# Reciprocals of the softmax sums as scaled fp16 pairs, one context piece loaded to another place, and a new order of work

## The reference

```
x = x + tanh(g_xattn) * ( softmax(mask(q kT * 64^-0.5)) v @ W_o + b_o )
      q = layernorm(x) @ W_q ; k = ctx @ W_k ; v = ctx @ W_v ; 8 heads of 64
x = x + tanh(g_ffn) * ( bitlinear(gelu(bitlinear(layernorm(x), w1, b1)), w2, b2) )
bitlinear(x, w, b): rmsnorm(x) rounded to 8 bits by its row's maximum,
                    w rounded to -1, 0, 1 by mean(|w|), product scaled back, + b
```

## Time and profile before

| | |
|---|---|
| time, median of 3 runs | 1135.02 us (1132.27 to 1136.66) |
| the profiled execution | 1132.84 us, span 1131.0 us |
| PE busy | 1033.3 us (91% of the span) |
| DVE busy | 909.8 us (80%) |
| POOL busy | 862.6 us (76%) |
| ACT busy | 794.7 us (70%) |
| DMA queue of the kernel | 74.6% of 16 engines |

### The profile page before, as it was taken

The page is one execution under the profiler, slowest core; times in us unless marked ns, Lnnn a source line. Parts: engine busy times, 40 slices in busy tenths (PEclk is TensorE's granted clock), DMA queues, the critical chain, the costliest instruction groups (busy, mean ns, idle before and its releaser), DMA issues.

```text
span 1131.0 us, 23832 instructions
## 1 busy us (share of the span) xinstructions
PE 1033.3 (91%) x8372; PEld 610.6 (54%) x8372; DVE 909.8 (80%) x1768; ACT 794.7 (70%) x1389; POOL 862.6 (76%) x767
## 2 busy tenths in 40 slices
...
GB/s 258 256 188 157 198 108 176 136 166 143 152 161 126 194 130 129 148 154 181 119 179 132 154 149 138 173 120 182 128 157 133 154 185 106 138 132 131 141 61 65
DMA packets 480005, 170.77 MB, mean 151 GB/s; under 512 B 458256, under 2 KB 460048, under 8 KB 479504
## 3 DMA queue, kind: packets, MB, share of 16 engines
q1 hardware_dynamic: 479888, 169.25, 74.6%
...
...
## 4 chain that ended last, share of the span: by engine, by line
PE 55%; POOL 16%; DVE 10%; issue 8%; DMA 6%; ACT 4%; SPq 1%; DVEq 0%; ACTq 0%; POOLq 0%
PE ps_g L544 29%; POOL p L984 8%; PE ps_g L641 7%; PE ps_g L597 6%; PE ps_s L574 6%; PE ps_g L633 5%; DMA hqt<-hq 4%; POOL p L979 2%; PE ps_g L585 2%; DVE prob L701 2%; DVE hq L835 1%; DVE xa L744 1%; ACT prob L881 1%; DMA xt<-xh 1%; POOL h_sb L1047 1%
## 5 line engine op out<-in xcount | busy, mean ns | idle before, releaser
L984 POOL TENSOR_TENSOR p<-prob,p 112x750 f16<-112x750 f32 x256 | 416.4, 1638 | 9.0 <-ACT p L888 4.9
L701 DVE CUSTOM_DVE_ANT_0 prob<-ps_s,mbias 112x750 f32<-112x750 f32 x256 | 235.6, 930 | 55.8 <-PE ps_s L574 52.9
L881 ACT ACTIVATE prob<-prob,rmin 112x750 f32<-112x750 f32 x256 | 233.6, 913 | 26.1 <-DVE rmin L701 25.8
L544 PE MATMUL ps_g<-ctx,wk 128*128 128x375 f16 x1152 | 203.2, 327 | 19.8 <-POOL ctx L995 18.1
L544 PE MATMUL ps_g<-wv,ctx 128*128 128x512 f16 (+1 forms) x864 | 204.0, 382 | 9.2 <-POOL ctx L995 6.2
L574 PE MATMUL ps_s<-k_sb,q_sb 64*112 64x375 f16 x1536 | 150.2, 328 | 17.0 <-DVE rmin L701 16.7
L544 PEld LDWEIGHTS ps_g<-ctx,wk 128*128 128x128 f16 x1152 | 108.3, 98 | 105.3 <-issue 35.5
L544 PEld LDWEIGHTS ps_g<-wv,ctx 128*128 128x128 f16 (+1 forms) x864 | 88.5, 104 | 96.5 <-issue 9.3
L888 ACT ACTIVATE p<-prob 112x750 f16<-112x750 f32 x160 | 129.5, 819 | 5.5 <-DMA pt<-p 4.6
L574 PEld LDWEIGHTS ps_s<-k_sb,q_sb 64*112 64x112 f16 x1536 | 90.5, 127 | 74.6 <-issue 41.9
L979 POOL CAST p<-prob 112x750 f16<-112x750 f32 x96 | 104.2, 1086 | 28.1 <-ACT prob L881 27.9
...
## 6 DMA issues: line engine op xcount, KB each, us to landing
...
pt<-p SPq DMA_TRANSPOSE x256, 3.9
...
```

The costliest lines, as they stand in the source:

```text
L544: mm = nc.tensor.matmul(out, lhs, rhs, start=(m == 0), stop=(m == len(steps) - 1))
L701: nc.vector.tensor_tensor_reduce(prob[:, (b * NU + n) % PROBS, :].rearrange("p (c k) -> p c k", c=2), ps_s[0:HT, n % 2, :, 0:CH], mbias[:, ...
L881: nc.scalar.activation(prob[:, (b * NU + n) % PROBS, :], prob[:, (b * NU + n) % PROBS, :], ACT.Exp, bias=rmin[:, n:n + 1], scale=-1.0, acc ...
L984: nc.gpsimd.tensor_tensor(p16[:, u % HILO, 1, 0:J], prob[:, (b * NU + n) % PROBS, :], p16[:, u % HILO, 0, 0:J], ALU.subtract).then_inc(s[" ...
```

## The change

Four things change.

1. `R:n` is now four per batch instead of eight. Each takes four reciprocals and then writes them, times 1024, as an fp16 high half and an fp16 low half (`rr16`). That is three dependent DVE instructions instead of one, each waiting for the one before it by a semaphore.
2. `PV:n` spreads the two halves instead of the one fp32 number: eight fp16 products that add up in pairs, instead of four fp32 products. The identity is fp16 and holds 1/1024.
3. The third context piece of batch 0 goes into a free part of `pt`, with a semaphore of its own, and no longer waits for POOL.
4. All tables of the order are new.

```
-                    nc.vector.reciprocal(rrec[:, 2 * n:2 * n + 2], rsum[:, 2 * n:2 * n + 2])\
-                        .then_inc(s["recips"], 1)
+                    of = slice(4 * n, 4 * n + 4)
+                    need(dve, "expd", b, 4 * n + 3)
+                    need(dve, "weighted", b - 1, n)
+                    nc.vector.reciprocal(rrec[:, of], rsum[:, of]).then_inc(s["recips_f"], 1)
+                    need(dve, "recips_f", b, n)
+                    nc.vector.tensor_scalar(rr16[:, 0, of], rrec[:, of], RS, None, ALU.mult).then_inc(s["recips_hi"], 1)
+                    need(dve, "recips_hi", b, n)
+                    nc.vector.scalar_tensor_tensor(out=rr16[:, 1, of], in0=rrec[:, of], scalar=RS, in1=rr16[:, 0, of],
+                                                   op0=ALU.mult, op1=ALU.subtract).then_inc(s["recips"], 1)
...
                     for m in range(2 * n, 2 * n + 2):
                         at = 256 + half_of(b, m) * HT
-                        for e in range(2):
-                            nc.tensor.matmul(g[e * DH:(e + 1) * DH, at:at + HT],
-                                             rrec[:, 2 * m + e:2 * m + e + 1].to_broadcast([HT, DH]),
-                                             ident[0:HT, 0:HT], start=True, stop=True)
+                        for a in range(2):
+                            for e in range(2):
+                                nc.tensor.matmul(g[e * DH:(e + 1) * DH, at:at + HT],
+                                                 rr16[:, a, 2 * m + e:2 * m + e + 1].to_broadcast([HT, DH]),
+                                                 ident[0:HT, 0:HT], start=(a == 0), stop=(a == 1))
...
+        def ctx_place(c):
+            return pt_words[:, 3 * WCH:3 * WCH + J] if c == KC - 1 else ctx_f[:, c % 2, :]
...
-                    need(sp, "ctx_lo", 0, c - 2)
-                    sp.dma_start(ctx_f[:, c % 2, :], ctx_d[b, :, n, :]).then_inc(d_ctx[c % 2], 16)
+                    if c >= KC:
+                        need(sp, "ctx_lo", 0, c - 2 if c > KC + 1 else 1)
+                    sp.dma_start(ctx_place(c), ctx_d[b, :, n, :]).then_inc(d_ctx[2 if c == KC - 1 else c % 2], 16)
...
 START = listed("""
-    MB:0:0 PW:0:0 CX:0:0 LC:0:0 CX:1:0 PD:0:0 N1:0:0 XN:0:0 XH:0:0 LC:1:0 LM:0:0 LX:0:0 XH:1:0 PD:1:0 CX:2:0 PW:1:0
+    CX:0:0 N1:0:0 LX:0:0 XN:0:0 LC:0:0 CX:1:0 PW:0:0 XH:0:0 XH:1:0 CX:2:0 PW:1:0 K:0:0 N1:0:1 KL:0:0 KL:1:0 XN:0:1
```

More of the change, by code:

```diff
@@ L46 @@
 VS = 8.0
+RS = 1024.0
 QSCALE = -(DH ** -0.5) / WS
@@ L137 @@
[L137 to L151, removed]
@@ new lines @@
+    Q:1:0 KL:3:0 PD:2:0 XH:1:1 WB:0:0 LX:0:1 M:1:0 WA:1:0 WA:2:0 K:4:0 XT:0:0 KL:4:0 S:0:0 XT:1:0 V:0:0 LM:0:0
+    WB:1:0 WA:3:0 M:2:0 E:0:0 L:0:0 WL:0:0 WA:4:0 WL:2:0 WB:2:0 WL:1:0 VL:0:0 E:1:0 VL:1:0 K:5:0 WL:3:0 M:3:0
+    WL:4:0 WL:5:0 WA:5:0 S:1:0 KL:5:0 WL:6:0 L:1:0 KL:6:0 LX:0:2 V:1:0 WL:7:0 WB:3:0 E:2:0 WA:6:0 K:6:0 WA:7:0
+    V:2:0 WM:0:0 PD:3:0 LC:0:1 VL:2:0 E:3:0 WL:8:0 H:0:0 PW:3:0 H:1:0 K:7:0 V:3:0 WQ:0:0 KL:7:0 WR:0:0 LC:1:1
+    BD:0:0 WB:4:0 WR:1:0 V:4:0 WR:2:0 WL:9:0 WR:3:0 WQ:1:0 V:5:0 WR:4:0 WQ:2:0 CX:0:1 CX:1:1 E:4:0 WB:5:0 WQ:3:0
@@ new lines @@
+    M:4:0 Q:2:0 WL:12:0 S:2:0 WL:15:0 WA:8:0 VL:3:0 N1:0:2 H:2:0 WB:6:0 WA:9:0 WL:10:0 M:5:0 WL:13:0 WG:0:0 E:5:0
+    WR:5:0 LC:2:1 WL:11:0 Q:3:0 L:2:0 WA:10:0 S:3:0 WQ:4:0 WB:7:0 S:4:0 WQ:5:0 H:3:0 QL:2:0 CX:2:1 WR:6:0 WA:11:0
+    M:6:0 WR:7:0 WA:12:0 WA:13:0 L:3:0 M:7:0 WL:14:0 WQ:6:0 V:0:1 T:0:0 VL:4:0 VL:5:0 L:4:0 H:4:0 XN:0:2 K:0:1
+    K:1:1 T:1:0 XT:0:1 QL:3:0 H:5:0 WA:14:0 VL:0:1 M:8:0 M:9:0 S:5:0 R:0:0 KL:0:1 WM:1:0 KL:1:1 QL:0:1 WA:15:0
+    M:10:0 R:1:0 T:2:0 WQ:7:0 XT:1:1 M:11:0 VL:1:1 E:6:0 WQ:8:0 E:7:0 QL:1:1 T:3:0 VL:2:1 M:12:0 H:6:0 T:4:0 WR:8:0
@@ new lines @@
+    L:5:0 LM:0:1 M:13:0 Q:0:1 LC:0:2 T:5:0 WB:8:0 H:7:0 Q:1:1 E:8:0 T:6:0 WB:9:0 L:6:0 T:7:0 R:2:0 H:8:0 WB:10:0
+    E:9:0 WB:11:0 PA:0:0 V:1:1 T:8:0 WQ:9:0 V:2:1 H:9:0 T:9:0 PV:0:0 L:7:0 L:8:0 L:9:0 WB:12:0 WQ:10:0 KL:2:1 S:6:0
+    E:10:0 WR:9:0 H:10:0 T:10:0 WR:10:0 E:11:0 E:12:0 M:14:0 K:2:1 K:3:1 T:11:0 WQ:11:0 L:10:0 WB:13:0 M:15:0
+    WR:11:0 S:7:0 H:11:0 K:4:1 L:11:0 KL:3:1 WQ:12:0 M:0:1 KL:4:1 PA:1:0 E:13:0 WR:12:0 H:12:0 MB:0:1 PV:1:0 L:12:0
+    E:14:0 QL:2:1 PL:0:0 WQ:13:0 M:1:1 T:12:0 BD:1:0 R:3:0 H:13:0 E:15:0 L:13:0 WB:14:0 Q:2:1 T:13:0 WB:15:0
@@ L156 @@
+    WR:13:0 S:0:1 E:0:1 KL:5:1 H:14:0 PL:1:0 K:5:1 H:15:0 WQ:14:0 WR:14:0 L:14:0 H:0:1 M:2:1 VL:3:1 V:3:1 KL:6:1
+    E:1:1 PA:2:0 L:15:0 K:6:1 M:3:1 V:4:1 VL:4:1 E:2:1 L:0:1 L:1:1 LR:1:0 S:1:1 M:4:1 PV:2:0 M:5:1 KL:7:1 H:1:1
+    XH:0:2 PA:3:0 K:7:1 T:14:0 XH:1:2 CX:0:2 V:5:1 T:15:0 T:0:1 WQ:15:0 LM:0:2 PL:2:0 E:3:1 WR:15:0 LC:1:2 H:2:1
+    XB:1:0 S:2:1 VL:5:1
 """, 0)
@@ new lines @@
+    PL:0:-1 H:9:-1 L:7:-1 E:10:-1 M:10:-1 T:6:-1 T:7:-1 F1:2:-2 GE:0:-2 F1:3:-2 GS:0:-2 R:1:-1 LR:0:-1 T:8:-1
+    L3:1:-2 L:8:-1 M:11:-1 H:10:-1 XQ:1:-2 T:9:-1 T:10:-1 S:6:-1 L4:1:-2 E:11:-1 PV:1:-1 H:11:-1 L:9:-1 T:11:-1
+    L:10:-1 S:7:-1 HT:0:-2 GM:0:-2 G2:0:-2 M:12:-1 GI:0:-2 M:13:-1 PA:1:-1 L:11:-1 L:12:-1 G3:0:-2 M:14:-1 R:2:-1
+    E:12:-1 H:12:-1 M:15:-1 F1:4:-2 F1:5:-2 R:3:-1 E:13:-1 H:13:-1 E:14:-1 F1:6:-2 F1:7:-2 T:12:-1 T:13:-1 T:14:-1
+    L:13:-1 PA:2:-1 PL:1:-1 L:14:-1 H:14:-1 T:15:-1 E:15:-1 LR:1:-1 PV:2:-1 F2:0:-2 H:15:-1 L:15:-1 GE:1:-2 PL:2:-1
@@ L173 @@
+    GM:1:-2 HT:1:-2 XB:0:-1 G2:1:-2 GI:1:-2 GS:1:-2 PV:3:-1 PL:3:-1 XQ:0:-1 PA:3:-1 GE:0:-1 G3:1:-2 O:0:-1 XB:1:-1
+    L2:0:-1 L3:0:-1 O:1:-1 L4:0:-1 XQ:1:-1 L2:1:-1 GS:0:-1 L3:1:-1 L4:1:-1 GE:1:-1 F2:1:-2 F1:0:-1 F1:1:-1 F1:2:-1
+    HT:0:-1 F1:3:-1 F1:4:-1 F1:5:-1 F1:6:-1 F1:7:-1 GM:0:-1 G2:0:-1 HT:1:-1 GI:0:-1 GM:1:-1 G2:1:-1 G3:0:-1 G3:1:-1
+    F2:0:-1 GI:1:-1 GS:1:-1 F2:1:-1
 """, NB)
```

47 lines of the change are left out of this document (16 added, 31 removed), and 57 rows, old and new, of tables (SLOTS, STAGE_OF_ITEM).

## The result

The changed kernel takes 1151.2 us (median of 4 runs, 1149.4 to 1157.3) against 1135.8 us before: a ratio of 1.015, 95% interval 1.011 to 1.020. It is slower by some 15 us, where 8 us less was forecast. The profiled execution of the changed kernel is the 1157.3 us one (span 1155.5), so it shows a few us more than the median does.

What follows compares the result with a forecast made beforehand. TensorE was taken to set the pace of the two-tile batches. Terms of -8.5, +4.5, -2 and -2 summed to -8.0 us, from 1132.8 to 1124.8 for the profiled execution, median 1127 us, range 1116 to 1142.

Steps and rivals of the forecast that it cites:

- the order in the middle: New item order in the middle batches: costed at nothing, as TensorE's items keep nearly the same neighbours.
- What bounds the kernel: Eleven two-tile batches between 1 and 14: TensorE sets the pace, busy 65.56 of a 65.65 us period.
- Term 1: TensorE's products spreading the reciprocals: fp16 takes 0.27 us a unit instead of 0.43, 8.5 us less (0 to 13).
- third of the rivals: Spread products on TensorE: an fp16 pair still takes 0.10 us, so no gain there; 1135.5 us, chance 0.10.
- Term 2: VectorE's new fp16-half operations, stretched beside GpSimd: 0.4 us a two-tile batch, 4.5 us more in all (0 to 19).
- VectorE becomes the bound: Two-tile batches: reciprocal items stretched by 1.6 us make VectorE set a 67.2 us period; 1146.5 us, chance 0.18.
- Term 3: Start: third context piece issued earlier, first product near 14.5 us, 3.5 sooner; 2 us less (0 to 4).
- Term 4: Last batch: `M:14` straight after `G3`, hidden rows' transpose sooner; 2 us less (4 less to 1 more).

Runs made afterwards that it cites:

- experiment 2: The changed kernel with fp32 reciprocals and spread products; new orders, four-column items and context place stay: 1110.9 us (0.978).
- experiment 4: The changed kernel without VectorE's computation of the low halves, which are set to zero once; TensorE's products stay: 1104.5 us (0.972).
- experiment 8: The changed kernel with one fp16 reciprocal straight from VectorE and one product in place of a pair, no low half: 1099.1 us (0.967).
- experiment 1: The changed kernel with only VectorE's item `R:3` moved behind `PA:2` in the last row of the order table: 1121.6 us (0.987).
- experiment 9: The changed kernel with the low half's operation replaced by a same-size reciprocal that nobody reads, low halves zero: 1105.6 us (0.974).
- experiment 5: The kernel before with only the first batch's third context piece loaded to its own place at once: 1135.05 us (0.999).

## Why the prediction was wrong, point by point

From the runs, before to changed: 2 us less by merging the items, 22 less by the new orders (with the context place), 40 more by the pairs. My sum had 0 for the order in the middle, -4 for start and tail, and -4 for the pairs (-8.5 and +4.5). So two terms were far off, in opposite directions, and the 15 us in the result are what is left of them.

**What bounds the kernel.** That TensorE sets the pace was right. The step from there was not: "its 0.1 us of idle in a two-tile batch leaves nothing to win". That row is of one batch. Over 900 us the same show 27.5 us of TensorE idle, and four other batches in a row show 8.5. The new orders take the 900 us to 10.4 us of idle and the four batches to 1.9. I had the number and read the neater row. So a term that was put at nothing measured some 20 us. Which of the orders' moves does it was not tried; of the waits above, the largest that goes is that for the transposed hidden rows (3.9 to 0.3 us), then those for `q_sb` (1.1 to 0) and for the transposed rows of x (1.7 to 0.8).

**Term 1, the products: right in the unit.** A spread unit was forecast at 0.27 us and takes 0.23. The third of the rivals (no shorter spread) is out. The estimate that the prediction made by the Trainium skill's page "TensorE: Matmul & The Clock Gate" (0.37 a unit) is too high for these 112-column products:

```profile
434.71 0.39 PE L596 MATMUL ps_g<-ident,rr 112*64 112x112 f16 x8
434.94 1.89 PE L608 MATMUL ps_g<-pt,v_sb 128*64 128x224 f16 x36
```

64 times 0.20 is 13 us at most. What the shorter units give in time no run has by itself; it is at least the 6.4 us between experiments 2 and 4, since experiment 4 also carries the high halves. Halving the products again (experiment 8) gave 5.4 us more, with the high half's cost inside it.

**Term 2, the halves on VectorE: the step that failed.** The mechanism stood in it, with its rows and the rule of the Trainium skill's page "SBUF — State Buffer" (section "Who interferes with whom"), which this trace bears out down to four columns (34 of 34 low halves that began beside a GpSimd operation were held). The price of an item was not far off: I gave it 0 to 1.1 us of stretch; over batches 1 to 14 an item's two halves last 1.37 us in the mean, 1.04 more than their shortest (0.17 and 0.16). What failed is how that becomes time. First, it is not even: `R:3`'s halves last 0.41 and 2.55. I had let each operation wait for the rest of one GpSimd operation, which is also how that page of the Trainium skill has it; `R:3`'s low half waited for two in ten of fourteen batches. Second, I turned the stretch into time through VectorE's load and its waits in a batch (66.7 us against TensorE's 65.0, at the most), and took 0.4 us a batch. It acts at a place: experiment 1 leaves the load no lower and moves one item, and 30 us go. Third, I listed what stands behind `R:0` and `R:1`, and not behind `R:3`: `KL:6`, `PA:2`, and through the bank `Q:2`. TensorE waits there 30.8 us and runs part of the next products at 1.2 GHz. Of the forecast's waits for `k_sb` or `v_sb` only 1.0 us came between 120 and 1060 us. The term was 4.5 us; the low halves' computation alone measured 46.7 (1151.2 less 1104.5), and as much by experiment 9.

**The rival "VectorE becomes the bound"** gave 1146.5 us, near the 1151.2 measured, but by luck: it had the orders at nothing. It is not what happened. The mean stretch stays under the 1.45 us an item from which it was to decide, and VectorE is busy 768 of 900 us. The remaining 17 us between experiment 1 (1121.6) and experiment 4 (1104.5) may well be such stretches of the other items in places that cost less; no run separates them.

**Term 3, the start.** The first product at 14.6 us, forecast about 14.5. The 2 us did not follow from it. The place alone gives nothing (experiment 5). With the new orders and fp32 TensorE has done 88 products by 30 us, against 66 before; by 60 us it is 224 in both, and by 120 us 659 against 662. The lead is used up by then, with the granted clock at 0.95 over those 60 us against 1.00 (before, then experiment 2):

```profile
0.00:30.00 30.00, 11.69 (x66) 6.84 (x68) 13.69 (x22) 13.87 (x19) 10.85 (x19) 1.00 0.82 267
0.00:60.00 60.00, 36.37 (x224) 20.28 (x224) 35.56 (x63) 42.66 (x69) 25.06 (x30) 1.00 0.75 253
```

```profile
0.00:30.00 30.00, 14.58 (x88) 8.70 (x89) 18.74 (x28) 16.16 (x22) 11.31 (x19) 1.00 0.85 283
0.00:60.00 60.00, 37.43 (x224) 21.43 (x224) 37.84 (x60) 43.25 (x70) 27.34 (x29) 0.95 0.77 261
```

**Term 4, the tail.** Forecast at 2 us less. With the new orders and fp32, 20 of the 22 us are there by the first context unit of the last batch (1019.3 us against 1039.9), and from there to the end it takes 90.0 us against 91.2: the tail gives some 1 us. The waits for the hidden rows fell from 24.1 to 15.5 us, with one of 13.2 left.
